# A fused vision and text network on one core: the opening reordered, later text rows moved into the first unit

## The reference, cut to what matters

```python
gray = jnp.einsum('bchw,c->bhw', x, w)[:, None]
edges = jax.lax.conv_general_dilated(gray, scharr, (1, 1), padding='SAME', ...)
edge = jnp.sqrt(jnp.square(edges)).sum(axis=1) / 2          # rows 0 to 255
idx = bigram_hash(x_txt, 262144)
text = jnp.einsum('bsd,md->bsm', embed_weight[idx], proj_weight) * scale   # rows 256 to 383
h = jnp.concatenate([edge, text], axis=1)
h = h + attn(layernorm(h))      # layer norm, qkv, rope on q and k, 16 heads of 16, softmax, Wo, then an MLP
h = h + ffn(layernorm(h))       # W1 and W2 rounded to -1, 0, 1 by their mean absolute value
```

## Time and profile before

| | us |
|---|---|
| median of 3 runs (lowest to highest) | 1967.54 (1960.39 to 1968.27) |
| profiled execution | 1963.76 |
| its span | 1962.0 |
| PE, DVE, ACT, POOL busy | 90%, 63%, 49%, 28% |

### The profile page before, as it was taken

The page is one execution under the profiler, slowest core; times in us unless marked ns, Lnnn a source line. Parts: engine busy times, 40 slices in busy tenths (PEclk is TensorE's granted clock), DMA queues, the critical chain, the costliest instruction groups (busy, mean ns, idle before and its releaser), DMA issues.

```text
span 1962.0 us, 35687 instructions
## 1 busy us (share of the span) xinstructions
PE 1771.4 (90%) x10970; PEld 1409.3 (72%) x10970; DVE 1236.2 (63%) x4035; ACT 963.8 (49%) x2657; POOL 543.5 (28%) x763
## 2 busy tenths in 40 slices
PE   5687999999999999899999999981499999999997
PEld 3455677676768677677777777761399998999896
DVE  6577677686777675756766776647745454545442
ACT  1355647474666666655566656540133334333431
POOL 2241423324232410111111111110424244434431
PEclk8698999999999999999999999995689999999998
DMA  6111010101001010103000010011213221221210
GB/s 204 38 36 63 1 61 0 59 1 60 32 11 56 2 33 2 33 1 91 18 15 32 32 32 24 1 43 65 84 39 111 94 76 46 79 76 64 61 39 21
DMA packets 74179, 90.05 MB, mean 46 GB/s; under 512 B 16524, under 2 KB 64311, under 8 KB 74073
## 3 DMA queue, kind: packets, MB, share of 16 engines
q1 hardware_dynamic: 61464, 67.88, 10.6%
q0 software_dynamic: 9472, 16.77, 3.0%
q10 hardware_dynamic: 3136, 4.21, 0.6%
HBM read 71.00 MB, written 25.00 MB: 49 GB/s over the span
## 4 chain that ended last, share of the span: by engine, by line
PE 74%; issue 10%; DVE 7%; POOL 2%; DMA 2%; ACT 1%; DVEq 1%; POOLq 1%; SPq 0%; ACTq 0%
PE bank L1002 17%; PE bank L1554 17%; PE bank L1569 9%; PE bank L950 6%; PE bank L934 6%; PE bank L985 6%; PE bank L906 3%; PE bank L1161 2%; PE bank L1024 2%; PE bank L961 1%; DVE probs L2229 1%; PE bank L891 1%; PE bank L907 1%; DVE at_least L2831 1%; PE bank L1537 1%
## 5 line engine op out<-in xcount | busy, mean ns | idle before, releaser
L1677 ACT ACTIVATE probs<-probs,nmax 128x128 f32<-128x128 f32 (+2 forms) x768 | 381.1, 502 | 66.4 <-DVE nmax L2229 66.2
L950 PE MATMUL bank<-cst,probs 128*128 128x128 f32 x1536 | 235.4, 280 | 18.2 <-ACT probsT L1685 8.4
L950 PEld LDWEIGHTS bank<-cst,probs 128*128 128x128 f32 x1536 | 183.2, 143 | 67.3 <-issue 22.1
L1554 PE MATMUL bank<-xeT,gate_w 128*128 128x480 f32 x768 | 188.5, 381 | 1.4 <-issue 1.4
L1554 PE MATMUL bank<-xeT,up_w 128*128 128x480 f32 x768 | 187.2, 379 | 0.0
L2324 DVE COPY probsT<-bank 128x384 f32<-128x384 f32 x256 | 141.3, 552 | 69.6 <-PE bank L950 68.4
L1569 PE MATMUL bank<-down_w,hT 128*120 128x256 f32 x1536 | 182.9, 281 | 0.0
L1569 PEld LDWEIGHTS bank<-down_w,hT 128*120 128x120 f32 x1536 | 181.6, 182 | 0.1
L1685 ACT COPY probsT<-bank 128x384 f32<-128x384 f32 x256 | 121.7, 475 | 117.4 <-PE bank L950 108.7
L3085 POOL COPY rinv<-rowsum 128x384 f32<-128x384 f32 x80 | 40.7, 509 | 499.1 <-DVE o1T L2251 294.8
L2978 DVE TENSOR_TENSOR prod<-bank,sil 128x480 f32<-128x480 f32 x128 | 83.8, 657 | 150.0 <-PE bank L1554 149.8
(11 more groups left out here) (320 smaller groups left out, 3324.4 us busy)
## 6 DMA issues: line engine op xcount, KB each, us to landing
gate_raw<-in_L_ffn_gate_w SPq DMA_DIRECT2D x8, 1024.0 KB, 4.9
up_raw<-in_L_ffn_up_w SPq DMA_DIRECT2D x8, 1024.0 KB, 6.9
down_raw<-in_L_ffn_down_w SPq DMA_DIRECT2D x8, 1024.0 KB, 5.7
img<-in_x SPq DMA_DIRECT2D x8, 768.0 KB, 5.1
residual_rows<-x SPq DMA_DIRECT2D x8, 384.0 KB, 2.5
residual_rows<-h_in SPq DMA_DIRECT2D x8, 384.0 KB, 3.8
xr<-residual_rows SPq DMA_DIRECT2D x8, 384.0 KB, 4.6
hr<-residual_rows SPq DMA_DIRECT2D x8, 384.0 KB, 3.6
```

Source lines behind the costliest of these rows:

```text
L950: last = tr(ps[bank][:, P * q:P * (q + 1)], probs[:, n % 4, SEG[t] + P * j:SEG[t] + P * (j + 1)], ident)
L1554: last = mm(ps[bank][:, 0:HALF], w[:, wp, c, P * m:P * (m + 1)], xeT[:, xp, c, HALF * hf:HALF * (hf + 1)], start=(c == 0 and k == 0), stop ...
L1677: last = f(p, p, ACT.Exp, bias=nmax[:, n % 4, t:t + 1], scale=-1.0, accum_out=rowsum[:, where, t:t + 1])
```

## The change

- The halo rows come in two transfers, each with three shifted copies of a row through an overlapping access pattern, in every unit; the semaphore counts 32 for an image in place of 96.
- `stay_warm(n)` on PE: n identity matmuls into an unused part of bank 5, seven places, without a wait: eight calls ahead of the first convolution, four behind gamma, eight behind the hash transpose, two after each text transpose and product, four before `qk_0`, eight before the first stacks and eight behind the first scores. Gamma moves ahead of the hash.
- Text rows 2 to 7 move from the opening into unit 0, in pairs: behind `values(1)`, behind `turn(1)`, and behind `turn(3)`. Their tiles move to another place in SBUF. ACT takes them behind exponentials 1, behind `take_turned(1)` and behind `take_first`. `store_texts` moves behind both spills of sequence 1 and waits for the last of them.
- Stacks are passed on by tile: ACT copies q and k of a tile as soon as it is roped (`first_roped`), DVE subtracts per tile, PE waits per tile and operand (`first_stacked`). POOL ropes tile 2, with its own scratch tile.
- ACT does the exponentials of head 0 in the opening. DVE's steps are in another order: hash_i ahead of the edge sums, thresholds behind the first normalisations, signs ahead of the last one, the ternary sum (2048 elements) near the end of the opening; masks of heads 0 and 1 ahead of the second half of the stacks.
- POOL gathers text 0 only before the first deviations; one gather follows each pair, and four stand behind its rope.

```diff
     if k.layer == 0:
         add(True, "v0_0", "v0_1")
+        add_texts(0)                       
+        add(k.s2, "proj0_0")
+        add_texts(1)
...
+WARM = (8, 4, 8, 2, 4, 8, 8)
...
 load_halo:
                 for k, row in enumerate((P - 1, 0)):
-                    for dx in range(3):
-                        sp.dma_start(halo_gray[dx:dx + 1, k, :], gray[row:row + 1, k, dx:dx + IMG]) \
-                            .then_inc(halo_loaded, 16)
+                    src = gray[row:row + 1, k, 0:IMG]
+                    shifted = bass.AP(src.tensor, src.offset, [src.ap[0], [1, 3], [1, IMG]])
+                    sp.dma_start(halo_gray[:, k, :], shifted).then_inc(halo_loaded, 16)
...
 SP:
             load_text(1)
-            store_texts()
             spill(1, 0)
             spill(1, 1)
+            store_texts()
             unit(0, U_FIRST)
...
 PE:
+            def stay_warm(n):
+                for _ in range(n):
+                    mm(ps[5][:, S:512], ident, ident, start=True, stop=True)
...
+                if sec == PRO:
+                    pe.wait_ge(first_stacked, 2 * NT * hh + 2 * t + (1 if x == "q" else 2))
...
                 def attn_rows(t):
+                    if k.tail is None:
+                        if t == 0:
+                            pe.wait_ge(emb_loaded[2], 16 * (B - 2))
+                        for b in (2 + 2 * t, 3 + 2 * t):
+                            text_columns(sec, b)
+                        for b in (2 + 2 * t, 3 + 2 * t):
+                            text_product(sec, b)
...
             banks.wait_taken(pe, SETUP, "projT")
             pe.wait_ge(edge_ready, 1)
+            stay_warm(WARM[0])
             convolve(SETUP, 0, (None, 0), range(2))
...
             convolve(PRO, 0, (None, 1), (1,))
-            pe.wait_ge(emb_loaded[2], 16 * (B - 2))
-            for b in range(2, B + 1):
-                if b < B:
-                    text_columns(b)
-                if b > 2:
-                    text_product(b - 1)
+            stay_warm(WARM[5])
...
 ACT, unit 0:
                     exps(1)
+                    take_texts(0)
                     exps(2)
                     take_turned(1)
+                    take_texts(1)
                     exps(3)
                     take_turned(2)
                     take_second()
                     take_first()
+                    take_texts(2)
                     exps(4)
...
 ACT, opening:
             for hh in range(2):
-                stack_upper_half((None, 0), hh, PRO, 0)
+                first_upper_half(hh)
+                if hh == 1:
+                    exps_of(0, 0, (None, 0))
...
 DVE, opening:
             for t in range(NT):
                 queries_keys_of(PRO, 0, t)
+            for t in range(NT - 1):
                 rope_of(t)
+            then()
+            v.nop().then_inc(roped, NT - 1)
             edges(PRO, 0, two, 0)
+            first_lower_half(0, 0)
+            first_lower_half(0, 1)
             edges(PRO, 0, two, 1)
+            first_lower_half(0, 2)
+            for t in range(NT):
+                take_stack_of(PRO, 0, 0, t)
             first_moments_of(two, 0)
             first_moments_of(two, 1)
+            for n in range(2):
+                mask_max_of(0, n, one)
+            for t in range(NT):
+                first_lower_half(1, t)
             first_norm_of(two, 0)
             first_norm_of(two, 1)
             for t in range(NT):
+                take_stack_of(PRO, 0, 1, t)
             first_moments_of(two, 2)
+            ternary_sum(0)
             first_norm_of(two, 2)
             for t in range(NT):
                 attn_norm_of(two, t)
...
 POOL, opening:
+            gather_text(1)
             for t in range(2):
                 inverse_deviation(LN_ATTN0, one, mv_a, rstd_a, t)
+            gather_text(2)
+            inverse_deviation(LN_FIRST, one, mv_a, rstd_a, 2)
             gather_text(3)
-            inverse_deviation(LN_FIRST, one, mv_a, rstd_a, 2)
             inverse_deviation(LN_ATTN0, one, mv_a, rstd_a, 2)
-            gather_text(4)
             pool.wait_ge(rows_loaded, 16 * ROW_LOADS)
             residuals(one)
-            for b in range(5, B):
+            rope_of(PRO, 0, NT - 1, rot2_first)
+            for b in range(4, B):
                 gather_text(b)
```

More of the change, by code:

```diff
@@ L232, in psum_plan @@
         bank_of = {name: 6 + k % 2 for k, name in enumerate(dense_units(like))}
+        bank_of.update({f"{name}{b}": 6 + b % 2 for name in ("embT", "txt") for b in range(2, B)})
         units.append([(name, bank_of[name], 1) for name in dense_units(kind)])
@@ L1413, in _ @@
             pe.wait_ge(edge_ready, 1)
+            stay_warm(WARM[0])
             convolve(SETUP, 0, (None, 0), range(2))
+            pe.wait_ge(abs_ready, 1)
+            k = banks.bank(SETUP, "gamma")
+            banks.wait_free(pe, SETUP, "gamma")
+            mm(ps[k][:, 0:2], const_cols("ones"), absum, start=True, stop=True).then_inc(filled[k], 1)
+            stay_warm(WARM[1])
             pe.wait_ge(hash_ready, 1)
@@ L1446, in _ @@
                     pair_scores(0, 0, (None, 0))
+                    stay_warm(WARM[6])
             taken(PRO, 0, f"stk1_{NT - 1}_q", f"stk1_{NT - 1}_k")
@@ L1642, in stack_upper_half, with first_upper_half, exps_of @@
                 last.then_inc(stack_hi, 1)
+            def first_upper_half(hh):
+                if hh == 1:
+                    banks.wait_filled(act, PRO, f"stk0_{NT - 1}_k")
+                for t in range(NT):
+                    if hh == 0 and t < NT - 1:
+                        act.wait_ge(first_roped, t + 1)
+                    elif hh == 0:
+                        act.wait_ge(roped, NT)
+                    for x, dst in enumerate((stk_q, stk_k)):
+                        o = dst[:, t].rearrange("p (h s d) -> p h s d", h=8, s=4)
+                        o = o[:, :, 0:4:2, :] if x == 0 else o[:, :, 0:2, :]
+                        src = qk[:, t, D * x + P * hh:D * x + P * (hh + 1)].rearrange("p (h d) -> p h d", h=8)
+                        nc.scalar.copy(o, src.unsqueeze(2).to_broadcast([P, 8, 2, HD0])).then_inc(first_upper, 1)
+                nc.scalar.nop().then_inc(stack_hi, 1)
+            def exps_of(layer, n, u):
+                s = n % 2
+                act.wait_ge(freed[s], at(u, PAIRS, take0[s] + n // 2 + 1))
+                where = sum_place(layer, n)
+                for t in range(NT):
+                    p = probs[:, n % 4, seg(t)]
+                    last = f(p, p, ACT.Exp, bias=nmax[:, n % 4, t:t + 1], scale=-1.0,
+                             accum_out=rowsum[:, where, t:t + 1])
+                last.then_inc(exp_done, 1)
             def take_stack_of(sec, i, hh, t):
@@ L1669, in exps, with take_texts @@
                 def exps(n):
-                    s = n % 2
-                    act.wait_ge(freed[s], at(u, PAIRS, take0[s] + n // 2 + 1))
-                    where = sum_place(k.layer, n)
-                    for t in range(NT):
-                        p = probs[:, n % 4, seg(t)]
-                        last = f(p, p, ACT.Exp, bias=nmax[:, n % 4, t:t + 1], scale=-1.0,
-                                 accum_out=rowsum[:, where, t:t + 1])
-                    last.then_inc(exp_done, 1)
+                    if k.tail is not None or n > 0:
+                        exps_of(k.layer, n, u)
+                def take_texts(t):
+                    if k.tail is None:
+                        for b in (2 + 2 * t, 3 + 2 * t):
+                            take_columns(sec, b)
+                        for b in (2 + 2 * t, 3 + 2 * t):
+                            take_text(sec, b, txt_rows[:, b, :])
                 def take_turned(n):
@@ L2735, in _ @@
             for t in range(NT):
-                take_stack_of(PRO, 0, 0, t)
-            stack_lower_half(one, 1)
+                take_stack_of(PRO, 0, 1, t)
             first_moments_of(two, 2)
-            banks.wait_taken(dve, SETUP, f"txt{B - 1}")
-            for n in range(2):
-                mask_max_of(0, n, one)
+            ternary_sum(0)
             first_norm_of(two, 2)
             for t in range(NT):
-                take_stack_of(PRO, 0, 1, t)
-            for t in range(NT):
                 attn_norm_of(two, t)
+            then()
+            v.nop().then_inc(stack_ready, 2)
             unit(SEC_FIRST, 0, (None, 0), U_FIRST)
```

113 lines of the change are left out of this document (63 added, 50 removed).

## The result

The changed kernel takes 2003.9 us (median; 2000.1 to 2011.1), the one before 1964.6 (1960.4 to 1968.3) beside it: a ratio of 1.0211, 95% interval 1.0188 to 1.0234. It is slower, by 2.1%, well clear of the noise (whether by more than 2%, the interval leaves open); the forecast was no change, 1967.5, with a range up to 1981. The profiled execution took 2007.7 us, its span is 2005.8.

| stretch | before | forecast | after |
|---|---|---|---|
| start to end of first convolution | 33.15 | 29.3 | 29.5 |
| to first `qk` product | 21.6 | 19.0 | 25.0 |
| to first scores | 30.3 | 21.5 | 21.7 |
| to second scores | 11.6 | 11.0 | 11.8 |
| to the load of `xr`, 183.70 and 207.27 | 87.0 | 106.5 | 119.2 |

The account below looks back on a forecast made before the run. PE, busy for 90% of the span, was taken as the bound, with holes at the start and at the change from attention to experts. 1963.8 - 15.8 (opening) + 19.5 (unit 0) = 1967.5 us; range 1951 to 1981.

Parts of the forecast that it names:

- First convolution: Opening, up to the first convolution's end: eight added calls raise PE's clock earlier, end at 29.3 us, -3.8 us.
- Convolution to first product: Opening, chain of DVE and POOL with PE waiting: 21.6 us becomes 19.0, -2.6; bounds -4.1 and 0.
- Product to first scores: Opening, ropes and stacks: ACT free, tile 0's stacks built meanwhile; 30.3 us becomes 21.5, -8.8; bounds -12.6 and -6.3.
- Unit 0: Second scores to unit 1: longer by DVE's tail, texts, late halo and clock, +19.5 us; bounds +12 and +26.
- (a): Unit 0: DVE's tail behind the last key eviction delays masks, values and the first moved text, +6.1 us.
- (c): Unit 0: the rows' store now precedes text load and halo 2 on SP; PE stands 5.3 us at the convolution.
- (b): Unit 0: three pairs of texts with PE and ACT handovers; +6.5 us at full clock, +9.8 at half, +7 taken.
- (d): Unit 0: PE stops twice and half clock costs something, 0 to 5 us, 1.1 taken; +5 by the skill's transpose rule.
- Everything from about 181 us on: Kernel behind the opening and unit 0: unchanged, merely earlier or later, so no change in length.
- The clock doesn't follow: Rival, opening and unit 0: added matmuls don't raise PE's clock; 1979.0 us, slower; chance 0.19.
- Absorbed: Rival, unit 0: texts, halo wait and clock, 13.4 us, vanish in slack; 1954.1 us, faster; chance 0.26.
- Not passed on by tile: Rival, opening's stacks: POOL's rope ends so late that all three tiles wait; 2.9 us more, 1970.4; chance 0.10.

Follow-up runs that it names:

- The run with the old order: Changed kernel with 12 no-operations on DVE, text 1's gather back right behind text 0's on POOL: 1975.4 us.
- with the halo early: Changed kernel with 12 no-operations on DVE, image 2's halo ahead of the text rows' store on SP, texts still in unit 0: 1976.0 us.
- the texts' place: Changed kernel with 12 no-operations on DVE, texts 2 to 7 moved from unit 0 to behind the first scores: 1965.9 us, ratio 1.0012.
- 12 nops: Changed kernel with 12 no-operations at the head of DVE's list, nothing else: 1987.2 us, 1.0128 of before.
- 55 in place of 46: Kernel before with no-operations on DVE while it waits for the hash transpose: 1975.5 us with 55, 1945.4 us with 46.
- the reordering itself: Changed kernel with early text 1 gather and hash, moved signs and texts, short DVE tail: 1949.3 us with 20 no-operations on DVE, 1936.5 with 65.

## Why the forecast failed, step by step

*First convolution*: end 29.5 against 29.3, by partly other means. ACT's copy of projT ended a microsecond later than assumed, at 17.6, and the clock rose at once with the convolution. The 3.8 us are there between the two profiles; that the calls earn them is not shown, since the clock also rose without them. The number was right by luck: a slow first convolution before, and not the calls, made the difference.

*Convolution to first product*: 19.0 forecast, 25.0 measured, wrong in sign. The step that failed is "Gone from it are DVE's sum of 2048 elements, 2.32 us, and one text gather ahead of the first deviations." I counted what the gather's removal saved and not what stands behind its new place: PE waits in order for text 1, 4.8 us with the clock gone behind it, and POOL's next drain holds it for 3.6 us, until a gather has landed that shares the DMA engines with an image load; before, the drains behind gathers held it for 1.07 and 1.41. "The shorter halo issue" was put at nothing, and it brings that load nearer. The run with the old order has the product 4.6 us earlier than the profile; its 21.0 us are still 2 above the forecast.

*Product to first scores*: 21.7 against 21.5, in part by two misses that cancel. POOL's rope was over at 66.1, and what the stacks waited for was DVE:

```profile
64.60 1.54 POOL L3154 TENSOR_TENSOR qk<-qk,rot_first 128x512 f32<-128x512 f32 x1
```

```profile
67.80 0.69 DVE L2272 TENSOR_TENSOR qk<-qk,rot 128x512 f32<-128x512 f32 x1
...
69.04 0.42 DVE L2340 TENSOR_TENSOR stk_q<-qk,stk_q 128x256 fp32r<-128x256 f32 x1
```

```profile
69.51 1.12 PE L1048 MATMUL bank<-ident_r,stk_q 128*128 128x128 f32 x4 [3.58 <-DVE stk_q L2340]
```

The last rope ended 14.0 us behind the product, not 15.6: DVE's two and POOL's one together took 7.8 us, more than the 4.7 of DVE's two alone and less than the 9.1 of full blocking. From there to the first scores it took 7.7 in place of 5.9, with an edge sum ahead of the subtractions on DVE. Passing on by tile did little: ACT had tile 0's copies at 65.8, but DVE's subtraction of tile 0 stands behind its rope of tile 1. What was gained is mainly that ACT was free of the texts, for which DVE waited 5.9 us before. *First to second scores*: 11.8 against 11.0; the calls ran at half clock, but without them it took 12.3.

*Unit 0*: +19.5 forecast, +32.2 measured (119.2 - 87.0). (a) DVE's tail and (c) the halo stand were right: 6.1, and 4.6 against 5.3 (by (c)'s own terms, 6.7 less the 1.96 covered, it would have been 4.7). (b) From the first text's transpose (100.52) to the third tile's `qk_0` (116.32) it took 15.8 us against 4.4 before, +11.4 where 7 was taken; it ran at half clock, for which the prediction had 9.8. (d) is the term that was mis-sized: 1.1 us taken, 0 to 5 as bounds, 9.6 measured in the profile (22.4 - 12.8) and 1.7 to 5.4 in six others. I let it be small because "much of the stretch waits for ACT anyway", which is true of the stretch of texts and false behind the stand, where 12.8 us of dense matmuls have nothing to wait for. The Trainium skill, "TensorE: Matmul & The Clock Gate", section "Part 4: PE-mode transpose", was cited for +5; what cost these 9.6 us was the stand and not the transposes, since with the halo early the same transposes and texts led into 12.8 us at full clock. Whether the half clock among the texts (0.50 from 100 to 110 us) is due to transposes or to waits, no run tells apart.

*Everything from about 181 us on*: "is as it was, merely earlier or later" is the step that cost most, 18.5 us in one loop and 1.7 elsewhere. Two rows of before spoke against it and were not read: DVE's issue gap of 3.3 us in a first-attention unit, and the packets of the instruction queue in three of them.

```profile
DVE rowsum L2245 <- issue: 3.3, 1, 3.3
```

```profile
q14 instruction: 17, 0.14, 0.2%
```

*The rivals.* "The clock doesn't follow" was the right side for another reason: the clock did rise in the first convolution, with the calls and without, and a late transfer lowered it in unit 0. "Absorbed" is refuted by the texts' place being worth 21 us. "Not passed on by tile" named the wrong engine (POOL's rope was over 2.4 us before DVE's), and its 2.9 us more did not come.

What stays open: why a stand at the same place costs between 1.7 and 9.6 us of clock, and why the first convolution's clock rose after 4 us in one execution and not in 15 in another. Runs of one kernel differ there, and no run here controls it. The change of the halo to two transfers was not undone alone, nor was the image load moved away from text 1's gather.

## What to carry to other kernels

Before trusting "the rest is unchanged", look at where each engine's loops lie in its instruction list: a few instructions more ahead of a loop moved this kernel by 17 us (12 nops) and by 30 (55 in place of 46), as much as the reordering itself or more, and padding with a few no-operations during a wait is the cheapest gain found here (-0.8% on the kernel before). When work is moved on an in-order queue, price what will stand behind it, gathers and stores above all, and not only what it leaves. A stand of PE of 4.6 us ahead of dense matmuls cost its own length and 1.7 to 9.6 us more in clock, so the late transfer is to be moved; filling the time showed no gain.

## What the hardware showed that I had not expected

DVE's loops run without a fetch in some places and with one in each pass in others. Loops (first instruction, length in the instruction list) at 1732/292, 1732/294, 1732/297, 1739/294, 1778/297, 1784/292, 1784/294, 1787/297, 588/366 and 597/363 ran free of it; 1720/292, 1824/292, 1848/297, 533/363, 542/366, 545/363, 552/363, 637/363, 658/366 and 597/366 did not. All of it fits blocks of 128 instructions that begin 64 to 66 past a multiple of 128, of which a loop may touch three; a fourth costs 2.7 to 6.6 us a pass in this kernel. Starts and lengths are counted in the built programs. One more row fits: DVE's second gap in the changed kernel's pass lies ahead of instruction 1730 of its list, 66 past a multiple of 128. The packets are of 8 KB; that each carries one such block is a conclusion, not shown. The Trainium skill, "Runtime: NRT & Kernel Launch", section "Instruction fetch mechanics", says that a taken branch to a target outside a window of two pages, 256 instructions each for these engines, forces a fetch before execution goes on. The runs agree that the branch back is what costs, and disagree on the size: the first loop is free only within a stretch that begins behind 545 and ends before 963, 417 instructions at the most, which is too small for two pages of 256. PE's loops are longer than DVE's, and moving them by 76 did nothing that could be measured.

A drain on POOL behind an indirect gather lasts until the gather has landed. The issue gap ahead of POOL's next step was 3.3 to 4.1 us for the gather of text 1 in its new place, and 1.07 and 1.41 us for two gathers of the kernel before; each time POOL went on 0.1 to 0.3 us behind the landing. A gather landed 2.4 to 2.8 us after its start where the DMA engines had little else, 4.4 to 5.2 beside the 768 KB image load, and 5.7 to 6.7 at 26 to 28 us, among the weight loads, in the kernels with the reordered opening.
